# Corrected rows scattered into memory and read back, one correction product per tile, the short tile in two transfers, and a rearranged start

## What is computed

```
# layer 0: attention over the pairs (sub, obj) that are edges of adj
q = x[sub] @ Wq.T + bq;  k = x[obj] @ Wk.T + bk           # 10000 pairs, 8 heads
scores = zeros(8, n, n); scores[:, sub, obj] = (q * k).sum(-1) / 8
scores = where(adj == 0, -inf, scores); diagonal = 1e-7
x1 = layernorm(x + softmax(scores).sum(heads) / 8 @ x)
# layer 1
out = layernorm(x1 + adj @ (x1 @ W) + bias)
```

## Time and profile before

| what | value |
|---|---|
| median of three runs | 191.53 us (191.08 to 191.73) |
| the profiled execution's own time | 191.3 us |
| its span from first to last instruction | 189.6 us |
| PE busy | 170.3 us, 90% |
| DVE, ACT, POOL busy | 117.7, 69.6, 71.2 us |
| granted TensorE clock, mean | 0.99 |
| bytes moved | 26.85 MB, mean 142 GB/s |

### The profile page before, as it was taken

One profiled execution on the slowest core, in us unless ns is written; L12 is line 12 of the kernel. 1 busy time (PEld: TensorE's weight loads), 2 busy tenths in 40 slices (PEclk: granted clock), 3 DMA queues, 4 the chain that ended last, 5 costly groups with the idle time before them and its releaser, 6 DMA issues.

```text
span 189.6 us, 2798 instructions
## 1 busy us (share of the span) xinstructions
PE 170.3 (90%) x1000; PEld 91.3 (48%) x1000; DVE 117.7 (62%) x358; ACT 69.6 (37%) x119; POOL 71.2 (38%) x83
## 2 busy tenths in 40 slices
PE   3889699999999999999999999995799999999910
PEld 3733156664544446544444469652456434444700
DVE  1999664868998774788114880658842118865660
ACT  7683468866344233342111125004222002433340
POOL 5588888787888756018740700000000000000000
PEclk9999999999999999999999999999999999999995
DMA  5999999994822288997110420000000000331220
GB/s 166 383 365 292 334 349 359 349 296 87 273 40 77 75 274 338 290 221 273 1 1 3 119 86 2 0 5 0 0 0 0 9 7 31 135 112 75 95 111 32
DMA packets 14567, 26.85 MB, mean 142 GB/s; under 512 B 5428, under 2 KB 5593, under 8 KB 14418
## 3 DMA queue, kind: packets, MB, share of 16 engines
q1 hardware_dynamic: 9150, 20.72, 32.2%
q10 hardware_dynamic: 3540, 4.84, 7.6%
q0 software_dynamic: 1856, 1.05, 4.4%
HBM read 16.89 MB, written 9.65 MB: 140 GB/s over the span
## 4 chain that ended last, share of the span: by engine, by line
PE 62%; DVE 10%; DMA 9%; POOL 5%; SPq 3%; issue 3%; ACT 3%; DVEq 0%
PE acc L1151 15%; PE acc L1303 11%; PE acc L1215 11%; PE tr L1151 8%; DMA stage<-in_adj_T 7%; POOL found L603 5%; PE tr L1261 4%; PE tr L1142 3%; PE tr L1303 3%; SPq L524 3%; PE acc L1315 2%; DMA found<-in_adj,top_i 2%; PE tr L1294 1%; PE tr L1165 1%; DVE st L817 1%
## 5 line engine op out<-in xcount | busy, mean ns | idle before, releaser
L585 POOL DMA_INDIRECT ed_adj<-in_adj,ed_idx x40 | 50.8, 1269 | 15.0 <-issue 11.9
L1215 PE MATMUL acc<-adjT,x1s 128*128 128x512 f16 (+3 forms) x264 | 53.0, 354 | 0.0
L1151 PE MATMUL acc<-xs,adjT 128*128 128x512 f16 (+1 forms) x176 | 40.7, 379 | 1.8 <-DVE xs L790 1.7
L1215 PEld LDWEIGHTS acc<-adjT,x1s 128*128 128x128 f16 (+1 forms) x264 | 25.0, 98 | 23.7 <-issue 1.4
L1151 PEld LDWEIGHTS acc<-xs,adjT 128*128 128x128 f16 (+1 forms) x176 | 16.3, 98 | 23.2 <-DVE xs L790 5.4
L1303 PE MATMUL acc<-whl,xs 128*128 128x512 f16 (+1 forms) x108 | 23.5, 367 | 0.0
L689 ACT ACTIVATE xs<-acc 128x512 f16<-128x512 f32 (+1 forms) x12 | 6.5, 545 | 26.1 <-PE acc L1215 26.0
L1303 PEld LDWEIGHTS acc<-whl,xs 128*128 128x128 f16 x108 | 10.6, 98 | 11.5
L603 POOL DMA_INDIRECT found<-in_adj,top_i x8 | 10.6, 1323 | 12.7 <-DVE top_i L929 10.6
L1151 PE MATMUL tr<-xs,adjT 128*128 128x512 f16 (+1 forms) x66 | 14.9, 379 | 0.0
L842 DVE SCALAR_TENSOR_TENSOR xs<-acc,xs 128x512 f16<-128x512 f32 (+1 forms) x12 | 7.4, 622 | 9.6 <-ACT xs L689 9.5
(11 more groups left out here) (240 smaller groups left out, 215.9 us busy)
## 6 DMA issues: line engine op xcount, KB each, us to landing
stage<-in_adj_T SPq DMA_DIRECT2D x6, 704.0 KB, 16.9
adjT_dram<-adjT SPq DMA_DIRECT2D x11, 352.0 KB, 2.7
x_sb<-in_x SPq DMA_DIRECT2D x10, 256.0 KB, 7.0
wraw<-in_adj_T SPq DMA_DIRECT2D x3, 704.0 KB, 16.0
sums_dram<-y ACTq DMA_DIRECT2D x6, 256.0 KB, 6.1
out<-y SPq DMA_DIRECT2D x6, 256.0 KB, 2.0
wT<-in_adj_T SPq DMA_DIRECT2D x2, 704.0 KB, 20.2
sums_dram<-xd ACTq DMA_DIRECT2D x5, 256.0 KB, 5.8
```

The costliest lines, as they stand in the source:

```text
L585: nc.gpsimd.indirect_dma_start(out=ed_adj[0:EP, c:c + 1], out_offset=None, in_=adj_flat, in_offset=bass.IndirectOffsetOnAxis(ap=ed_idx[0:E ...
L1151: last = mm(sum_bank(i)[:, :], adjT[0:width[k], k, i * P:(i + 1) * P], xs[0:width[k], half, k, :], start=(k == 0 and half == 0), stop=(k = ...
L1215: ins = mm(mix_bank(u)[:, 0:j - i], x1s[0:width[k], half, k, f * P:(f + 1) * P], adjT[0:width[k], k, i:j], start=(k == 0 and half == 0), s ...
```

## The change

These things change together.

1. x1 through memory: ACT stores each tile of x1 into `x1_dram`. When the slots' new rows are ready (q), POOL scatters them into `x1_dram` by an indirect transfer (rows that are not to be written get an index out of bounds), and SP then reads all eleven tiles back into `x_sb`.
2. The one-hot half of stackL goes. Both halves of stackL now hold the same adjacency columns, the upper half of stackR holds the low part and the lower half the high part, and `correct` is one product. For it, dx1 is transposed and multiplied for all 128 partitions. The bias, in a high and a low part, takes rows 63 and 127.
3. The short tile (74 rows) is loaded, reloaded and stored as 64 and 10 rows.
4. At the start, adjacency tile 0 is loaded and cast in two parts (5 and 6 blocks) with x tile 0 between them; PE starts with sums in place of `words(0)`; on DVE `split_x` comes before the rest, and the pairs' keys come later.
5. POOL looks up 44 columns in place of 40; one `look`, one `pick` and one `select` less.
6. Steps of the mix are moved ahead: five more before L1283, nine more in all before L1287.

```diff
-LOOKED = 40
+LOOKED = 44
-LOOKS_IN_MIX = {2: 8, 4: 9}
+LOOKS_IN_MIX = {2: 8}
-SELECTS_IN_MIX = {6: (6, 7)}
+SELECTS_IN_MIX = {5: (6, 7)}
...
             def load_adj(t):
...
+                if t == 0:
+                    sp.dma_start(adj_room(t)[:, 0:FIRST_BLOCKS * P], adj_t[t][:, 0:FIRST_BLOCKS * P]).then_inc(first_loaded, 16)
+                    load_x(0)
+                    sp.dma_start(adj_room(t)[:, FIRST_BLOCKS * P:NP], adj_t[t][:, FIRST_BLOCKS * P:NP]).then_inc(adj_loaded[t % RING], 16)
+                    return
...
             def load_x(t):
-                if t == T - 1:
-                    sp.wait_ge(pad_zeroed, 1)
-                sp.dma_start(x_sb[0:width[t], t, :], rows(x, t)).then_inc(x_loaded[t], 16)
+                if t < T - 1:
+                    sp.dma_start(x_sb[:, t, :], rows(x, t)).then_inc(x_loaded[t], 16)
+                    return
+                sp.wait_ge(pad_zeroed, 1)
+                for a, b in ((0, EVEN), (EVEN, LAST)):
+                    sp.dma_start(x_sb[a:b, t, :], x[t * P + a:t * P + b, :]).then_inc(x_loaded[t], 16)
...
+            sp.wait_ge(x1_lo, T)
+            sp.wait_ge(new_rows_in, 16)
+            for t in range(T - 1):
+                sp.dma_start(x_sb[:, t, :], rows(x1_dram, t)).then_inc(x_loaded[t], 16)
+            for a, b in ((0, EVEN), (EVEN, LAST)):
+                sp.dma_start(x_sb[a:b, T - 1, :], x1_dram[(T - 1) * P + a:(T - 1) * P + b, :]).then_inc(x_loaded[T - 1], 16)
             with overflow(sp):
                 general_sp(sp)
...
-                sp.dma_start(rows(out, t), y4(t)[0:width[t]]).then_inc(out_stored[t % 4], 16)
+                end = P if t < T - 1 else EVEN
+                sp.dma_start(out[t * P:t * P + end, :], y4(t)[0:end]).then_inc(out_stored[t % 4], 16)
...
-                out=stackL[0:BIAS_ROW, :], out_offset=None, in_=adjT_dram,
-                in_offset=bass.IndirectOffsetOnAxis(ap=slot_i[0:BIAS_ROW, 0:1], axis=0)).then_inc(cols_in, 16)
+                out=stackL[:, :], out_offset=None, in_=adjT_dram,
+                in_offset=bass.IndirectOffsetOnAxis(ap=cols_i[:, 0:1], axis=0), bounds_check=NP - 1, oob_is_err=False).then_inc(cols_in, 16)
+            pool.wait_ge(x1_stored, 16 * T)
+            pool.wait_ge(new_rows_ready, 2)
+            nc.gpsimd.indirect_dma_start(
+                out=x1_dram, out_offset=bass.IndirectOffsetOnAxis(ap=new_row_i[0:BIAS_ROW, 0:1], axis=0),
+                in_=q[0:BIAS_ROW], in_offset=None, bounds_check=N - 1, oob_is_err=False).then_inc(new_rows_in, 16)
...
                 nc.scalar.mul(x1s[:, 0, i, :], x_sb[:, i, :], XS).then_inc(x1_hi, 1)
+                act.dma_start(rows(x1_dram, i), x_sb[0:width[i], i, :]).then_inc(x1_stored, 16)
...
+            act.dma_start(out[N - LAST + EVEN:N, :], y4(T - 1)[EVEN:LAST]).then_inc(end_stored, 16)
...
+            dve.wait_ge(beyond_ready, 3)
+            V.tensor_tensor(cols_i[:], slot[:, 0:1], beyond[:], ALU.add).then_inc(cols_idx_ready, 1)
...
-            V.tensor_scalar(stackL[64:P, :], col_no[64:P, :], sub[64:P], None, ALU.is_equal).then_inc(low_ready, 1)
...
+                dve.wait_ge(x_loaded[t], 32)
                 V.scalar_tensor_tensor(y4(t), out_bank(t)[:, :], 1.0 / WS, x_sb[:, t, :], ALU.mult, ALU.add).then_inc(z_ready, 1)
...
-            mix_rows(85, 98)
+            mix_rows(85, 103)
...
-            mix_rows(98, 112)
+            mix_rows(103, 121)
...
-                for half in range(2):
-                    last = mm(bank, stackL[:, t * P:(t + 1) * P], stackR[:, half, columns], start=False, stop=(half == 1))
-                last.then_inc(out_done, 1)
+                mm(bank, stackL[:, t * P:(t + 1) * P], stackR[:, 1, columns], start=False, stop=True).then_inc(out_done, 1)
```

More of the change, by code:

```diff
@@ L14 @@
 LAST = N - (T - 1) * P
+EVEN = LAST // 16 * 16
+FIRST_BLOCKS = 5
 NP = T * P
@@ L397, in general_dve @@
             dve.wait_ge(based, EARLY)
+            dve.wait_ge(late_consts, 4)
+            for t in range(T):
+                dve.wait_ge(x_loaded[t], 32 if t < T - 1 else 64)
             dve.wait_ge(counts_stored, 16)
@@ L548, in _ @@
             sp.wait_ge(bias_split, 2)
-            sp.dma_start(stackR[BIAS_ROW:BIAS_ROW + 1, :, :], bias_hl[:, :, :]).then_inc(biased, 16)
+            for half in range(2):
+                bias_at = 64 * half + BIAS_ROW
+                sp.dma_start(stackR[bias_at:bias_at + 1, 1, :], bias_hl[:, half, :]).then_inc(biased, 16)
+            sp.wait_ge(x1_lo, T)
[4 more added lines that the diff above has]
+                sp.dma_start(x_sb[a:b, T - 1, :], x1_dram[(T - 1) * P + a:(T - 1) * P + b, :]).then_inc(x_loaded[T - 1], 16)
             with overflow(sp):
@@ L582, in _ @@
                            allow_small_or_imprecise_dtypes=True).then_inc(slot_consts, 1)
+            nc.gpsimd.memset(beyond[:], 0.0).then_inc(beyond_ready, 1)
+            for half in range(2):
+                pool.wait_ge(beyond_ready, 1 + half)
+                nc.gpsimd.affine_select(out=beyond[:], in_=beyond[:], compare_op=ALU.not_equal, fill=FAR,
+                                        base=-(64 * half + BIAS_ROW), pattern=[[0, 1]], channel_multiplier=1).then_inc(beyond_ready, 1)
             pool.wait_ge(idx_ready, 1)
@@ L598, in _ @@
                            allow_small_or_imprecise_dtypes=True).then_inc(late_consts, 1)
-            nc.gpsimd.memset(stackL[0:64, :], 1.0).then_inc(ones_laid, 1)
+            nc.gpsimd.memset(stackL[:, :], 1.0).then_inc(ones_laid, 1)
             pool.wait_ge(top_ready, 1)
@@ L645, in high_x @@
             def high_x(t):
-                act.wait_ge(x_loaded[t], 16)
+                act.wait_ge(x_loaded[t], 16 if t < T - 1 else 32)
                 nc.scalar.mul(xs[:, 0, t, :], x_sb[:, t, :], XS).then_inc(x_hi, 1)
@@ L655, in _ @@
             cast_adj(0)
-            for t in range(3):
+            for t in range(1, 3):
                 high_x(t)
@@ L736, in _ @@
                                      scale=st[:, t % 2, 8:9]).then_inc(z_normed, 1)
+            act.wait_ge(z_normed, T)
+            act.wait_ge(z_half_normed, 1)
+            act.dma_start(out[N - LAST + EVEN:N, :], y4(T - 1)[EVEN:LAST]).then_inc(end_stored, 16)
         @block.vector
@@ L845, in _ @@
             fits = slot[:, 8:9]
+            for t in range(3):
+                split_x(t)
             dve.wait_ge(consts, 4 + T)
@@ L851, in _ @@
             step(V.scalar_tensor_tensor(diag_bit, aii_all, -1.0, power, ALU.mult, ALU.mult))
-            for t in range(3):
-                split_x(t)
             split_left()
-            fold(0)
-            coefs(0, 1)
             for t in range(3, 9):
                 split_x(t)
+            fold(0)
+            for t in range(9, T):
+                split_x(t)
+            coefs(0, 1)
             fold(1)
@@ L861, in _ @@
             edge_bits()
-            for t in range(9, T):
-                split_x(t)
+            edge_keys()
             def add_sums(i):
@@ L1177, in _ @@
             pe.wait_ge(bit_eye_ready, T)
+            pe.wait_ge(first_cast, 1)
+            sum_neighbours(0, range(0, 3))
             words(0)
-            sum_neighbours(0, range(0, 3))
             words(1)
@@ L1226, in _ @@
             select(8)
-            select(9)
             mix_rows(11, 13)
```

76 lines of the change are left out of this document (46 added, 30 removed).

## The result

The change made the kernel slower: 194.39 us median (193.99 to 195.18, five runs) against 191.53 us of the kernel before on the same chip, ratio 1.0138 (95% interval 1.0094 to 1.0181). The forecast was 182.0 and the range ended at 185.0. The profiled execution took 195.18 us, with a span of 193.4.

The account below looks back on a forecast made before the run. PE, busy 170.3 of 189.6 us, was taken to bound the kernel through its start, work, waits and tail. 2.4 + 0.4 + 2.6 - 0.45 - 0.1 + 2.15 + 3.0 = 10.0, less 0.5, gave 182.0 us; range 180.5 to 185.0.

Parts of the forecast that it names:

- Lookups: Four more lookups on POOL stay hidden; PE saves 0.4 us, DVE 1.0; flags at 96.4, cover 0.7 us.
- a rival of 1 to 2 us: Late lookups, or adjT stores running into the flags' lookups, cost 1 to 2 us: 183 to 184; chance 0.1.
- the allowance of 0.5: 0.5 us taken off the summed gain for two chains, POOL's lookups and `hot`, with under 1 us of cover.
- Start: Rearranged loads and casts: `words(2)` near 20.8, first `look` near 53.4, gain 2.4 us, bounds 1.4 and 2.7.
- `hot`: Rival at the start: stores of x1 push `hot` later, start gives 0 to 1 us, 183.5 to 184.5; chance 0.2.
- PE's own work: Before the flags: PE finishes its filler at 97.1, from 99.90 less 2.4 and 0.4.
- Filler: Products moved ahead of the shares and dx1 fill 1.46 of 1.91 and 1.17 of 1.48 us: gain 2.6 us.
- Transposes: Transposes of dx1 double their columns, 0.46 us becomes 0.9: 0.45 us lost.
- Correction: At the end, ten tiles with one product less, 2.81 us a tile: gain 2.15 us.
- Reload: x1 scattered and read back before the first sum of the end, eight microseconds of cover: cost 0.
- The rival that was to make the kernel slower: First sum of the end waits for scatter and reload, a chain that would have to last 24 us; chance 0.03.
- Tail: Last store as 64 and 10 rows ends 3.0 us earlier, between 2.4 and 3.4.

Follow-up runs that it names:

- e7: The change with lookups 37 to 40 counted on a semaphore of their own, stores of adjT at the same point; one run, 190.25 us.
- e3: The change with POOL's col_no and stackL made ahead of the lookups; 194.52 us, ratio 1.0157 to the kernel before.
- e12: The change with adjT stored behind the slots' gathers, Wq and Wk loaded where those stores were; ratio 1.0490 to the kernel before.
- e14: The change (44 lookups, 36 on the first semaphore) with Wq/Wk early, POOL's preparation first, bias rows then adjT stores behind the gathers; 187.84 us, ratio 0.9769.
- e4: The kernel before with 44 lookups in place of 40, nothing else of the change; 198.07 us, ratio 1.0284.
- e8: The kernel before with only the short tile loaded and stored as 64 and 10 rows; 188.26 us, ratio 0.9752.
- e13: The change with 40 lookups, Wq/Wk early, POOL's preparation first, bias rows then adjT stores behind the gathers; 183.96 us, ratio 0.9593 to the kernel before.
- e5: The change with 44 lookups, stores of adjT after 28 lookups, POOL's preparation first; 187.01 us, ratio 0.9695 to the kernel before.
- e6: The change with 40 lookups, stores of adjT after 28 lookups, POOL's preparation first; 184.64 us, ratio 0.9576 to the kernel before.
- e2: The change with 44 lookups, stores of adjT after 36 of them in place of 40; 188.67 us, ratio 0.9822 to the kernel before.
- e11: The change with 50 extra products on PE ahead of its wait for the flags; 192.92 us, ratio 1.0089 to the kernel before.
- e15: The change with 42 lookups in place of 40 on the first semaphore, stores of adjT waiting for 42; one run, 194.93 us.
- e1: The change with 40 lookups and the look, pick and select of before, gate 36 again; 187.86 us median, no ratio.
- e10: The change with 40 lookups, Wq/Wk early, POOL's preparation first, adjT stores behind the gathers, bias rows behind those stores; ratio 1.0014 to the kernel before.

## Why the prediction was wrong

**The step that failed** is *Lookups*: "Four more on POOL cost 4 x (50.8 + 11.9) / 40 = 6.3 us ... so it is free at 80.4", with the flags at 96.4 and a cover of 0.7 us. It moved everything behind the lookups by POOL's issue time and kept their rate and landing as before. The flags came at 108.20, 11.8 us later, 7.8 ahead of `found` and 4.0 behind it:
- `found` started at 89.14 and not at 81.3. The last lookup was issued at 79.53, where 68.09 + 6.3 is 74.4: 3.2 us of that is the pause (3.5 in place of the usual 0.3, gone in e7), and 2.2 the sixth lookup, which took 3.68 us at 14.47 where that of before took 1.51. It also landed 2.5 us slower than before. With the old rate and landing it would have been there at 77.3, ahead of DVE, which was ready near 79.6; so DVE waited until 85.0. POOL's preparation, behind the same landing, fell on DVE's operations: 2.2 us by their rows (e3 shows it, and got 1.5 of it back).
- The flag chain took 19.1 and not 15.1 us: 3.4 us through the landing of the last one, beside the stores of adjT and the loads of W, and 0.5 because DVE's long operation now fell on an issue for longer. The stores were named ("if the stores of adjT, which SP starts four lookups later, run into the flags' lookups"), but in a rival of 1 to 2 us with a chance of 0.1. e12 shows their effect: with the stores behind the gathers, and the loads of W ahead, the chain is 15.5. Why the last lookup lands late is less clear: it does so with the stores away too (7.2 us in e12, 6.0 in e14).

The slow sixth lookup comes with the new start and not with the four lookups: one near 14 us takes 3.1 to 6.0 us in every kernel with the start rearranged, and none there takes over 1.7 in the kernel before, e4 and e8. What holds it is open: DVE's splits of x run beside it (13.38 to 17.06), but also beside the fifth of before (1.64 us).

On top come 2.9 us of lower clock, of which the prediction says nothing. Against the forecast of 181.8 for the profiled execution: PE was at the flags at 108.4 where I had 97.1, so 11.3, and 2.9 for the clock, less the allowance of 0.5, is 13.7; measured was 195.18 - 181.8 = 13.4. The 0.3 between them is the sum of smaller misses of both signs: what lies between the flags and the first `base` came out about 0.9 better than forecast, the correction about 0.1 and the tail 0.3 worse.

**The sign of this step was wrong too**: not a gain of 0.4 us with a hidden cost, but 3.3 us lost with the stores of adjT out of the way (e14 against e13), 2.3 with them early (e5 against e6), and 5.4 us on the kernel before (e4).

**What was right.**
- *Start*: `words(2)` at 21.38 (I had 20.8), the first `look` at 53.55, so 2.1 us earlier (I had 2.4); `hot` did not set the pace.
- *PE's own work*: its filler before the flags ended at 97.35 (97.1).
- *Filler*: no wait at the shares, 0.35 us at dx1; from the transposes to the first `base` 6.35 us in place of 8.82.
- *Transposes*: mis-sized; 0.66 for 128 columns against 0.46 for 64 is 0.2 lost, not 0.45.
- *Correction*: 2.81 us a tile, as worked out, though the stretch from the first `base` to the last `correct` is 2.0 us shorter and not 2.15.
- *Reload*: scatter at 148.82, reloads issued from 151.61 to 157.6, first sum at 163.90 with no wait for them. A reload took 4.8 us to land in the median, not 2.0; the cover of eight microseconds hid that. The rival that was to make the kernel slower had nothing to do with why it is.
- *Tail*: 2.8 us in place of 5.5, so 2.7 (I had 3.0). e8 shows it alone. The Trainium skill's rule against such a split ("DMA: Bandwidth & Descriptors", Rules for kernel authors) would have made this term nothing; it does not hold for 74 rows, by these numbers.

e13 is the check of the whole sum: it is the change without its part 5, with POOL's preparation and the loads of W early and the stores of adjT out of the way. Its profiled execution took 183.53 us, 1.7 above the forecast of 181.8, and PE waits 1.6 us at the flags.

What stays open: why a pause comes before the 40th lookup, why the last lookup lands late without the stores, the gaps of e5 and e6 near 46 and 56 us, and the nameless wait at the first `correct` (0.45 before, 0.57 to 1.84 in the others).

## What to carry to other kernels

Price a transfer that an engine waits for up to its landing, and read the landing at a time as crowded as the new one will be. When a constant changes, look for every place where it stands: here the same number gated 4 MB of stores on another queue, and its shift, with the pause that came along, cost 6 us (e2 against the change), more than the work it was changed for. A wait of PE can be paid again in the clock behind it (here 3.6 us of waiting cost 1.7 more, 11.1 us 2.9 more), so a chain with 0.7 us of cover is a risk of more than a microsecond for each microsecond. And when DVE's operations are moved, look at what POOL issues beside them.

## What the runs showed of the hardware

- Ahead of the 40th indirect transfer POOL stood still for 2.5 to 3.5 us in all six kernels that put 40 or more of them on one semaphore (the change, e3, e4, e11, e12, e15, the last with 42), and in none of those with 28 or 36 on the first one and 40 or 44 in all (before, e1, e2, e5 to e10, e13, e14). The count on one semaphore is shown to matter, the mechanism isn't.
- An indirect transfer whose issue began within DVE's operation of 2.28 us (128x2048, two inputs) was held until 1.07 to 1.09 us behind it, in all 17 kernels: 2.1 to 3.1 us in place of 1.2.
- Landings of lookups of 125 single values: 3.4 us with quiet DMA engines (e12), 7.3 to 8.7 us beside stores of 352 KB (e1, e3, e4, e7), medians of eight.
- A DVE operation of 0.17 us on 8 integers took 1.2 to 1.3 beside an iota or memset of POOL.
- The 14 products behind PE's wait for the flags took 3.18 us after a wait of 1.6 us (e13), 4.87 after 3.6 (e14) and 6.06 after 11.1. In between the price does not follow the length: 5.92 after 4.6 us (e2), 4.74 after 10.4 (e3).
